# Delta attention on one core: the five instruction queues of the main loop in another order

## The reference, cut to what matters

```
q, k, v = silu(causal conv of 4 taps (x @ W)),  k and v three per time step
S = S * exp(g_t);  for i in 0..2:  S += b_i * k_i (v_i - k_i S)
o_t = q_t S;  out = (rmsnorm(o) * silu(x @ Wg)) @ Wo
```

## Time and profile before

| | us |
|---|---|
| median of 3 runs | 3191.56 (3190.16 to 3193.73) |
| profiled execution, its own time | 3186.49 |
| its span | 3184.4 |
| PE busy | 2986.1 (94%) |
| DVE busy | 2530.9 (79%) |
| ACT busy | 2250.1 (71%) |
| POOL busy | 1977.0 (62%) |

### The profile page before, as it was taken

The page is one execution under the profiler, slowest core; times in us unless marked ns, Lnnn a source line. Parts: engine busy times, 40 slices in busy tenths (PEclk is TensorE's granted clock), DMA queues, the critical chain, the costliest instruction groups (busy, mean ns, idle before and its releaser), DMA issues. The chain is left out here.

```text
span 3184.4 us, 83423 instructions
## 1 busy us (share of the span) xinstructions
PE 2986.1 (94%) x27212; PEld 2356.1 (74%) x27212; DVE 2530.9 (79%) x5859; ACT 2250.1 (71%) x6955; POOL 1977.0 (62%) x3125
## 2 busy tenths in 40 slices
PE   5669999999999999999999999999988999867999
PEld 3458888888888888888888888888877444455444
DVE  5669999999999999999999999999855445585544
ACT  4768888888888888888888888888743444314443
POOL 1588888888888888888888888888851000100000
PEclk8779999999999999999999999999999899968999
DMA  5456777776767776767777767676732333002242
GB/s 108 121 154 167 191 180 182 172 181 170 181 172 189 177 178 174 185 167 182 174 185 178 185 171 178 176 180 168 184 96 64 129 148 130 30 3 73 108 160 113
DMA packets 588203, 482.87 MB, mean 152 GB/s; under 512 B 464784, under 2 KB 504368, under 8 KB 581632
## 3 DMA queue, kind: packets, MB, share of 16 engines
q1 hardware_dynamic: 579328, 474.39, 56.5%
q10 hardware_dynamic: 8448, 3.15, 0.4%
HBM read 285.53 MB, written 191.86 MB: 150 GB/s over the span
## 5 line engine op out<-in xcount | busy, mean ns | idle before, releaser
L931 DVE SCALAR_TENSOR_TENSOR conv_k<-PP,tk,conv_k 128x256 f32<-128x256 f32 x1536 | 722.7, 479 | 60.0 <-ACT conv_k L766 32.8
L704 POOL TENSOR_TENSOR X<-X,tmp 96x31 f32<-96x31 f32 (+15 forms) x992 | 534.8, 539 | 77.8
L931 DVE SCALAR_TENSOR_TENSOR conv_v<-PP,tv,conv_v 128x256 f32<-128x256 f32 x1152 | 539.3, 477 | 44.9 <-ACT conv_v L766 35.3
L701 POOL TENSOR_TENSOR tmp<-At,X 96x31 f32<-96x31 f32 (+15 forms) x992 | 486.3, 490 | 63.3 <-DMA At<-n_d 5.0
L1100 PE MATMUL PP<-xn,wk 128*128 128x268 f32 x1024 | 342.3, 418 | 38.0 <-DVE conv_k L931 26.3
L687 POOL TENSOR_TENSOR rk<-ss,half 96x8 f32<-96x8 f32 x128 | 209.1, 1634 | 175.2 <-DVE ss L899 175.2
L669 POOL TENSOR_TENSOR Sg<-S,gend 128x512 f32<-128x512 f32 x256 | 265.9, 1039 | 59.2 <-DVE S L890 59.2
L738 ACT ACTIVATE recA<-TG,es 96x128 f32<-96x128 f32 x1024 | 284.9, 368 | 5.1 <-DVE es L924 5.1
L766 ACT ACTIVATE conv_k<-PP,tk 128x256 f32<-128x256 f32 x512 | 245.3, 480 | 57.1 <-PE PP L1100 49.7
L730 ACT ACTIVATE recA<-TG 128x128 f32<-128x128 f32 x1024 | 265.5, 272 | 25.5 <-PE TG L1151 25.5
L1064 PE MATMUL RB<-rhs,Yf 96*96 96x128 f32 x2048 | 269.0, 274 | 14.5 <-DVE rhs L879 14.3
(11 more groups left out here) (291 smaller groups left out, 6735.0 us busy)
## 6 DMA issues: line engine op xcount, KB each, us to landing
kqg_d<-kqgA SPq DMA_DIRECT2D x128, 512.0 KB, 6.4
kqgB<-kqg_d SPq DMA_DIRECT2D x128, 512.0 KB, 4.5
rec_d<-recA SPq DMA_DIRECT2D x128, 480.0 KB, 3.4
recB<-rec_d SPq DMA_DIRECT2D x128, 480.0 KB, 6.0
f1gates<-f1gates_d SPq DMA_DIRECT2D x24, 1024.0 KB, 6.5
f2gates<-f2gates_d SPq DMA_DIRECT2D x24, 1024.0 KB, 6.8
gdec<-gdec_d SPq DMA_DIRECT2D x128, 128.0 KB, 5.8
apk_d<-apkA SPq DMA_DIRECT2D x128, 128.0 KB, 3.3
```

The costliest lines, as they stand in the source:

```text
L701: nc.gpsimd.tensor_tensor(t, At[q % 2][:, j, j + 1:].unsqueeze(2).broadcast_to(sh), X[q % 2][:, j, 0:cols].unsqueeze(1).broadcast_to(sh), ...
L704: nc.gpsimd.tensor_tensor(x, x, t, ALU.subtract).then_inc(sub_ev, 1)
L931: return nc.vector.scalar_tensor_tensor(acc, src[:, :, j:j + SPAN], w[:, j:j + 1], acc, ALU.mult, ALU.add)
```

## The change

The call orders of all five queues are written anew, and within them the stages are shifted against each other by whole steps: the key stage is at f - 1 instead of f, its second half at f - 2, the state stage at r - 1 and the output at r - 2, while the tiles of v stay at c and what follows from them is at c - 1. The loops run one step further (SP also begins one earlier). No operation, no buffer and no wait inside an operation changes.

```diff
 SP:
-            for f in range(NF):
+            for f in range(-1, NF + 1):
                 r, c = f - BACK - 1, f - BACK
+                dec_load(f - 1)
+                y_load(c)
+                ap_store(f - 2)
+                x_store(*group_at(f - 1, 2 * GROUP + 1))
+                rec_store(f - 2)
+                weights(*divmod(f + 1, KSTEPS))
+                da_load(c + 1)
+                rec_load(c)
                 at_load(*group_at(f, GROUP + 1))
-                x_store(*group_at(f, 2 * GROUP + 1))
-                rec_load(c)
-                da_load(c + 1)
-                weights(*divmod(f, KSTEPS))
-                dec_load(f)
-                kqg_store(f - 1)
-                rec_store(f - 1)
-                ap_store(f - 1)
-                y_load(c + 1)
+                kqg_store(f - 2)
 POOL:
-            for f in range(NF):
+            for f in range(NF + 1):
                 r, c = f - BACK - 1, f - BACK
-                x_zero(*group_at(f, 3))
+                sg(r - 1, 1)
                 fo_(r - 1)
-                kqg(f - 1)
+                kqg(f - 2)
+                rk_(f - 2)
                 sg(r, 0)
-                rk_(f - 1)
-                subst(*group_at(f, GROUP + 1), range(0, 6))
-                sg(r, 1)
-                subst(*group_at(f, GROUP + 1), range(6, 12))
+                subst(*group_at(f - 1, GROUP + 1), range(0, 6))
+                x_zero(*group_at(f - 1, 3))
+                subst(*group_at(f - 1, GROUP + 1), range(6, 12))
```

More of the change, by code:

```diff
@@ L841, in xt @@
                 nc.scalar.activation(At[q % 2][:, :, :], X[q % 2][:, :, :].rearrange("p r c -> p c r"), ACT.Copy).then_inc(xt_ev, 1)
-            for f in range(NF):
+            for f in range(NF + 1):
                 r, c = f - BACK - 1, f - BACK
-                xt(*group_at(f, 2 * GROUP + 1))
+                gate_(c - 1)
+                w12(c - 1)
+                tap0(f - 1, "k1")
+                tap0(f - 1, "k0")
+                wev(r - 1, 0)
+                ksum_(f - 2, 0)
+                ksum_(f - 2, 1)
+                vsilu(c - 1)
+                tap0(f - 1, "k2")
+                tap0(f - 1, "q")
+                kr(f - 2, 0)
+                yev(c - 1)
+                kr(f - 2, 1)
+                wev(r - 1, 1)
                 tap0(c, "v0")
                 tap0(c, "v1")
-                ksum_(f - 1, 1)
-                ksum_(f - 1, 0)
-                wev(r, 0)
-                tap0(c, "v2")
[L852 to L868, removed]
+                ksilu(f - 1)
+                mo_(r - 1, 0)
+                qsilu(f - 1)
+                q2_(f - 2)
+                mo_(r - 1, 1)
+                zev(c)
+                tap0(c, "v2")
+                xt(*group_at(f - 1, 2 * GROUP + 1))
         @block.vector
@@ L997, in _ @@
             dve.wait_ge(rms_ev, 1)
-            for f in range(NF):
+            for f in range(NF + 1):
                 r, c = f - BACK - 1, f - BACK
+                tap1(c - 1, "v2")
+                og_(r - 2)
+                tap2(c - 1, "v2")
+                tap3(c - 1, "v2")
+                rhs_(r - 1, 0)
+                tap1(f - 1, "k1")
+                tap1(f - 1, "k0")
+                tap2(f - 1, "k1")
+                tap2(f - 1, "k0")
+                tap3(f - 1, "k0")
+                tap3(f - 1, "k1")
+                sup(r - 1, 0)
+                ss_(f - 2)
+                rinv_(f - 2)
+                step_(f - 2)
+                acc_(r - 2)
+                es_(f - 2)
+                rhs_(r - 1, 1)
+                tap1(f - 1, "k2")
+                tap1(f - 1, "q")
+                tap2(f - 1, "k2")
+                tap2(f - 1, "q")
+                tap3(f - 1, "k2")
+                tap3(f - 1, "q")
+                ap(f - 2, 0)
                 tap1(c, "v0")
-                osb_(r - 1)
                 tap2(c, "v0")
-                rhs_(r, 0)
+                ap(f - 2, 1)
                 tap3(c, "v0")
                 tap1(c, "v1")
-                og_(r - 1)
+                vr(c - 1, 0)
                 tap2(c, "v1")
+                sup(r - 1, 1)
                 tap3(c, "v1")
[L1009 to L1035, removed]
+                osb_(r - 1)
+                vr(c - 1, 1)
         @block.tensor
@@ L1214, in out @@
                 mm(SD[:, 0:256], wo[N // KSTEPS % 2][:, :], og[:, :], start=True, stop=True).then_inc(out_mm, 1)
-            for f in range(NF):
+            for f in range(NF + 1):
                 r, c = f - BACK - 1, f - BACK
+                ks(r - 1, 0)
+                ot(r - 2)
+                gate_tile(c - 1)
+                wm(c - 1)
+                k_tile(f - 1, 1)
+                k_tile(f - 1, 0)
+                w_(r - 1, 0)
+                ktr(f - 2, 0)
+                ktr(f - 2, 1)
+                sr(r - 1, 0)
+                k_tile(f - 1, 2)
+                k_tile(f - 1, 3)
+                out(r - 2)
+                ks(r - 1, 1)
+                m3(c - 1)
+                o_(r - 1, 0)
+                w_(r - 1, 1)
+                gram(f - 2, 0)
                 v_tile(c, 0)
                 v_tile(c, 1)
-                ktr(f - 1, 1)
-                ks(r, 0)
-                ktr(f - 1, 0)
+                gram(f - 2, 1)
+                vtr(c - 1, 0)
+                sr(r - 1, 1)
+                o_(r - 1, 1)
                 zm(c)
-                ot(r - 1)
-                w_(r, 0)
                 v_tile(c, 2)
[L1227 to L1244, removed]
+                vtr(c - 1, 1)
 def normed_mixture(nc, g, tag, last=False):
```

## The result

The changed kernel takes 3197.98 us (median of 9 runs, 3193.94 to 3201.34) against 3190.16 of the kernel before on the same chip: a ratio of 1.0023, 95% interval 1.0012 to 1.0033. It is slower by a fifth of a per cent, where 35 us less were forecast.

What follows compares the result with a forecast made beforehand. PE sets the pace at 17.71 us a step; 17.71 - 0.05 + 0.08 - 0.14 = 17.60 gains 13 us over 116 full steps, the first steps 22: 35 off, 3157 us, range 3140 to 3172.

Steps and rivals of the forecast that it cites:

- Waits inside a full step: Full loop, engine queues against PE's new order: `sr` weights load late, 0.08 us more a step; other chains keep small margins.
- PE's own time: PE in a full step: fewer changes between small and large products, 0.05 us less; bounds none and 0.32.
- the section: `o_` with `zm` on PE: taken as not truly merged; rival that it merges, 0.32 off a step, 3126, chance 0.10.
- the small saving: PE's full step: 0.05 us less, since `o_` and `zm` differ in width and a tiling-mode change drains TensorE.
- `xt`: Copy at the end of ACT's queue: costs 0.2 in one of four steps, 0.05 a step instead of 0.19, 0.14 gained.
- The first steps: Ahead of the full loop: 22 us gained, 8.4 from turns of 9.1 and 14 behind `xt`; bounds 8 and 28.
- The last steps: Last twelve steps, same work without keys: costed at nothing, 0.3 us a step either way, 4 us in all.
- The slower rival: ACT's chain from `wev(.,0)` to `kr(.,0)` late, delaying `gram(.,0)`, v tiles, taps, `sup(.,1)`: 24 us more, 3216; chance 0.14.
- the signs announced: For: `ks` steps 17.5 to 17.6, first `ks` about 205; against: PE waiting over 0.3 us a step for ACT or DVE.
- Two signs of a right forecast: In the full loop: DVE busy less by a few per cent, and `ws` named as releaser of `sr`.

Runs made afterwards that it cites:

- experiment eleven: Changed kernel with `rk_(f - 2)` moved behind the first half of `subst` in POOL's queue and two buffers for `ss`: 3165.70 us, ratio 0.9929.
- experiment five: Changed kernel with `rk_` late and one unit younger, and `m3` moved ahead of `out` in PE's queue: 3261.63 us, ratio 1.0231.
- experiment one: Changed kernel with each product and difference of `subst` on POOL cut to one element a partition: 3173.05 us.
- three: Changed kernel with `rk_` moved behind the first half of `subst` and one unit younger (f - 1): 3175.41 us, ratio 0.9957.
- eight: Kernel of three with `rk_(f - 2)` early up to f = 13; last step: `ks(.,1)` before `out`, `o_(.,1)` before `sr(.,1)`: 3167.36 us, ratio 0.9936.
- ten: Kernel of nine; last step: `ks(127,1)` ahead of `out(126)`, `o_(127,1)` ahead of `sr(127,1)`, `rhs(127,0)` ahead of `og(126)`: 3700.01 us.
- nine: Changed kernel with `rk_(f - 2)` moved behind the first half of `subst` in POOL's queue, `ss` still one buffer: 3700.59 us, ratio 1.160.
- experiment seven: Changed kernel with `rhs_(.,1)` ahead of `es_` in DVE's queue: 3213.51 us, ratio 1.0080.
- experiment four: Kernel before the change with `rk_` moved to the end of POOL's step: 3210.26 us, ratio 1.0062.

## Why the prediction was wrong

- **The step that failed: "Waits inside a full step".** It priced DVE at 15.6 us of work with the durations of its operations taken as fixed (measured: 16.3 busy before and after, 16.0 in experiment eleven), checked `rhs_(.,0)`, and had no margin at all for `rhs_(.,1)` or for the taps of k2 and q that the v tiles wait for. POOL's new order was checked for its waits alone. In the changed kernel `ss`, `step_s` and `es` together take 0.35 longer than before (1.220 for 0.868 us, by the groups above), and the step is 0.29 over its forecast (17.894 for 17.60). That is 34 of the 35 us between -13 and +22. With the three at 0.875 (experiment eleven) the step is 17.632, 0.03 over the forecast. What runs beside an operation was in no term of the sum and in no rival.
- **PE's own time was right.** Without most of the holds the full step is 17.626 to 17.632, with many steps at 17.55. `sr` takes 0.97 to the next product (1164.95 to 1165.93) instead of 0.87, 0.10 more where 0.08 was taken, and `o_` to `zm` takes 0.60 (1174.64 to 1175.24) instead of 0.46 between equal widths, so the section doesn't merge in full. The trace agrees with the rule of the Trainium skill (TensorEngine Tiling (Array Packing), Key Properties) that a change of tiling mode drains TensorE, and my choice of the small saving holds. A section costs 0.29, by experiment five.
- **`xt` was right**: where it stands, a step of experiment eleven takes 17.75 to 17.79, others mostly 17.55 to 17.64, and part of that is the hold, which those steps still have; without it, in experiment one, it is 17.68 against 17.55, 0.13 where 0.2 was taken. Before, the step of `xt` was 0.74 longer.
- **The first steps gained 16.3 instead of 22.** `qsilu` and `subst` in them, changed kernel:

```profile
83.15 0.38 ACT L807 ACTIVATE kq<-conv_k 128x256 f32<-128x256 f32 x1
119.51 0.42 ACT L807 ACTIVATE kq<-conv_k 128x256 f32<-128x256 f32 x1
128.99 0.23 POOL L701 TENSOR_TENSOR tmp<-At,X 96x31 f32<-96x31 f32 x1 [1.76 <-DMA At<-n_d]
178.87 1.96 ACT L841 ACTIVATE At<-X 96x1024 f32<-96x1024 f32 x1 [3.00 <-POOL X L704]
```

  Four turns take 36.4, 9.09 each where I took 9.1, and the fifth `qsilu` is 8.7 ahead of that of before (128.26), where I took 8.4. But `subst` starts only 5.65 sooner (before: 134.64) and the first `xt` 5.6 sooner, since a unit's second half now lies deeper in the next turn, and the load of At takes 5.0 us from issue (123.94) instead of 3.4 (131.26). From the end of `xt` to the first `ks` it takes 30.4 where I took 27 and it was 41.1.
- **The last steps weren't free.** They cost 7.1, outside the 4 allowed. The 2.3 up to `ks` 127 is not told from the spread of that stretch (173.4 here, 172.0, 172.1 and 170.9 in experiments three, eight and eleven, 171.1 before). The 4.8 behind it can be followed in the trace, against the kernel before:
  - 1.4 of it lies ahead of `w_(127,0)`, which starts 3.27 after `ks` instead of 1.89. DVE waits for POOL's `fo_` at `osb_`, and the last `vr` and `rhs_(127,0)` stand behind that in the new order:

```profile
2461.59 0.42 DVE L978 TENSOR_TENSOR osb<-SD,fo 128x256 f32<-128x256 f32 x1 [1.46 <-POOL fo L680]
```

  - About 2 is the granted clock, which falls in the last step (windows; the first is of the kernel before, the second of the one after, columns as in the earlier trace rows):

```profile
2455.00:2460.00 5.00, 3.79 (x39) 2.78 (x37) 1.80 (x3) 0.96 (x3) 1.04 (x1) 1.00 0.02 3
```

```profile
2465.00:2470.00 5.00, 4.53 (x18) 3.88 (x18) 1.12 (x2) 0.42 (x1) 1.04 (x1) 0.52 0.00 0
```

  At 0.52 nearly all of that stretch is at the lower level, 1.2 of 2.4 GHz, and `sr` and `ks` take about twice as long:

```profile
2465.47 2.07 PE L1074 MATMUL RA<-ws,recB 96*128 96x128 f32 x8 [0.68 <-ACT ws L756]
2468.33 2.02 PE L1054 MATMUL RA<-S,kqgB 128*96 128x128 f32 x8
```

  Before, the same two took 1.16 and 1.11. PE was busy for 2.99 of the 5 us ahead of the fall (2460 to 2465); before, for 3.79 and 3.25 of the 5 us from 2455 and from 2460, at 1.0. Why the clock fell in one kernel and not in the other isn't shown.
  - The last 1.4 is from `w_(127,1)` to `ot` (5.98 instead of 4.55): `o_(127,1)` now stands behind `sr(127,1)`, which is 1.1, and the rest is still at the low clock. Experiments eight and ten put `o_` back and win that 1.1 (4.86 in ten, 5.91 in nine). But the same edit put `out(126)` behind `ks(127,1)`, and `acc_(126)`, which stands ahead of `rhs_(127,1)` in DVE's queue, then waits 2.97 for it: `ks(127,1)` to `w_(127,1)` takes 4.09 in ten and 2.98 in nine. The two moves cancel, which is why neither run gained.
- **The slower rival** named the right victims, `gram(.,0)` and the v tiles, and the right size (24 more; the loop lost 22), by the wrong cause: ACT's chain isn't late by itself. It becomes late when `es` does, in experiment seven.
- **Of the signs announced**, the first `ks` at "about 205" was 211, `o_` to `zm` was 0.60 where 0.46 or 0.56 was announced, and the one that would show it wrong, PE waiting for DVE, is what came: its weight loads waited 18.4 us at `rhs` and 9.2 at `conv_k` in 67 steps, 0.41 a step, mostly 0.2 to 0.3 us at a time. Two signs of a right forecast stayed out: DVE is busy for 16.3 us a step as before, not less by a few per cent, and no wait of `sr` for `ws` shows in these steps.

With most of the hold away (experiment eleven, against the profile of before) the spans differ by 20.8 us: 16.6 at the start, 8.5 in the loop, 0.2 up to `ks` 127 and 0.8 in the rest, less 5.4 at the end. So of the 35 forecast, 14 were wrong in the sum itself, and the hold took 30 more.

## What to carry to other kernels

An order of one queue also sets what runs beside what. With `ss` and `step_s` held for over 0.5 us together, a step of the old order got at most 0.1 longer (experiment four); in the new order 0.35 us of holds cost 0.26. So look at both: who is beside the operation, and how close behind it the busiest engine stands. Before moving an operation of DVE or POOL, list the DVE operations whose inputs all lie in SBUF, look in the trace at which POOL instruction runs beside each before and after, and price the ones on a tight chain with what that POOL instruction may have left; a queue with 1.4 us to spare in a step of 17.7 can still be late by 0.1 at the one place that counts. And when an operation is made later, look at who may not overwrite its input until it is done: a single small buffer, here 8 numbers a partition, can close a ring that costs 4.5 us a step.

## What the runs showed of the hardware

- A DVE operation of 0.16 us on 96 x 8 numbers takes 0.97 beside a POOL `tensor_tensor` of 1.04, and ends 0.02 us behind it, which is less than its own 0.16. `ss`, with one SBUF input and an SBUF output, is held as well (in the changed kernel up to 0.57 instead of 0.17); `rinv`, a reciprocal from SBUF to SBUF, never is (198 to 201 ns in every kernel, 28 times beside L701 in the changed one).
- POOL's `pow` (`rk_`, 1.64 us, two SBUF inputs) holds nothing: beside it `step_s` took 0.15 to 0.17 in all 68 cases before and in all 50 of experiment eleven, `ss` 0.17 in 33 and `es` 0.40 to 0.42 in 68 of experiment eleven. The rule of the Trainium skill cited above (SBUF — State Buffer, "SBUF: two separate sides") makes no such exception; here the measurement decides.
- The hold goes both ways: in the changed kernel POOL's L704 of 96x156 takes 0.55 or 0.56 in the 28 cases that began while `es` ran, as at 1168.52, and 0.49 to 0.51 in the other 36. In experiment one an instruction of POOL of 0.19 took 0.42 to 0.45 in the 49 cases where it began within 0.04 us behind the start of `es`, which takes 0.41, and ended 0.05 behind its end.
